# Pairing the state transposes and their additions in a software-pipelined Mamba and mixture-of-experts kernel, with the silu and softplus groups moved by a slot

## The chip, the cores and the metric

The kernel runs on one core of a Trainium2 chip. The metric is the device time of one execution in microseconds. All data are f32. The engines are named as in the profile: PE (TensorE, matrix products and transposes), PEld (its weight loads), DVE (VectorE), ACT (ScalarE), POOL (GpSimd) and SP (SyncE, which issues the transfers). Each runs its own list of instructions in order, and they wait for each other through semaphores.

## The reference

The input has 2 sequences of 4096 tokens of 256 values. One Mamba layer is followed by one mixture-of-experts layer, each with a layer norm before it, a layer norm behind it and a residual:

```
xz = einsum('bld,de->ble', layernorm(x), W_in); x_in, z = split(xz, 2)   # 512 channels each
u = silu(causal_conv4(x_in) + conv_b)
dt, B, C = split(u @ W_xproj, [16, 16, 16]);  delta = softplus(dt @ W_dt + b_dt)
h_t = exp(delta_t * A) * h_(t-1) + (delta_t * u_t) * B_t      # 512 channels x 16 states
y_t = sum over states of h_t * C_t
out = ((y + D_skip * u) * silu(z)) @ W_out;   x = x + layernorm(out)
...
x = x + layernorm(shared(x') + sum over the top 2 of 8 experts of coef * down(silu(gate) * up))
```

with x' the layer norm of x, 8 routed experts of width 128 and one shared expert of width 256 (two more blocks of 128, so 10 blocks f = 0 to 9).

## The kernel before

The tokens are cut into 16 chunks of T = 512, and a chunk into four quarters of 128 tokens. One pass of the loop over chunks has 64 slots (16 states times 4 blocks of 128 channels), and three chunks are in work in it: the scan of chunk s, the output projection and experts of chunk s - 1 (`ffn_part`), and the input projection, convolution, softplus and so on of chunk s + 1 (`prep_part`, `conv_part`). Every engine has its own loop over the slots t = 0 to 63. A table of slot numbers, written by hand, says in which slot an engine issues which piece, and so alone sets the order on each engine. Slots are places in these lists and no times: an engine may be a slot or more ahead of another, as far as the semaphores let it.

In each slot ACT makes one exponential d_a = exp(delta * A) (line 599), for the scan two slots later, since there are two PSUM banks for d_a. DVE runs one scan (line 757) for one state and 128 channels, and frees the bank. POOL makes d_bu for two slots at a time (line 1002).

The state h lies with channels on the partitions, and y is wanted with tokens there. So for each state n and quarter a (together q = 4n + a, 0 to 63 in a chunk) PE transposes four blocks of 128x128 into a PSUM bank `ht` (`transpose_state`, line 447), and DVE multiplies them by C and adds them to y_t (`add_state`, line 767). For q = 0 to 3 ACT does this instead (`first_state`, line 607, in its slots 5 to 8). There are two `ht` banks: the transposes of q wait for the addition of q - 2. Before the change PE transposes q in its slot q + 4, and DVE adds mostly one q in a slot. `LATER` names six slots with no addition and six, three slots on, with two.

Around this lie, in the order of a pass (the names are those of the table):
- y_t is transposed back (YD_PE, line 460), D_skip * u is added by DVE (YD_DVE), POOL multiplies by silu(z) (Y_GATE, line 1058) and PE projects (OUT_PE, line 471). DVE takes moments (O_STATS), adds the residual and takes moments again (X1_STATS). POOL makes the reciprocal deviation, ACT normalizes (line 616), PE transposes (X1T_PE, line 490) and ACT copies (line 656).
- PE projects the four blocks of x_in (XIN_PE, line 435). ACT takes the halo and the first tap (TAP0_ACT, lines 688, 692) and scales the taps of block 3 (line 700), DVE does the other taps of blocks 0 to 2 (CONV, line 924), POOL those of block 3 (line 1045), ACT the silu of u (SILU).
- The experts come in five pairs of blocks that start at PAIR_AT: two gates (line 509), then silu on ACT two slots later, the up products (line 516) three slots after the gates, the `hidden` products on POOL five slots after, the down products (line 536) later. An up product goes to the bank `ring` of its gate, which the silu frees. The last down product is in PE's slot 59, and DVE's moments of the expert layer's result (Y_STATS, slot 60) wait for it.
- DL_PE and DL_ACT are the product for delta and its softplus, Z_PE the product for z, CF_PE, CT_PE and XD_PE small ones. The next gate's bank is the one that a softplus frees.

Silu and softplus need another table on ACT than exp, so a group of them has an ACT_TABLE_LOAD ahead of it and one behind it.

Of the kernel before, what the change touches and what calls it, by code (L numbers as in the profile page):

```python
# [33 lines left out]
def mamba_moe_kernel(nc, x, w_in, conv_w, conv_b, w_xproj, w_dt, b_dt, a_log, d_skip, w_out,  # L34
# [10 lines left out]
    NT = T // P  # L45
    KM = DM // P
    J = DI // P
# [11 lines left out]
    with ExitStack() as ctx:  # L59
# [128 lines left out]


        SLOTS = NS * NT  # L190
        XIN_PE, TAP0_ACT, CONV = (5, 5, 8, 9), (5, 6, 9, 9), (7, 8, 11, 11)
        POOL_J, POOL_CONV = J - 1, 11
        YD_PE, YD_DVE, Y_GATE, OUT_PE = 3, 4, 5, (6, 6, 7, 7)
        O_STATS, X1_STATS, X1T_PE = 9, 10, 11
        PAIR_AT = (12, 21, 31, 41, 50)
        ROUTER_PE, ROUTE_DVE, ROUTE_EXP = 14, (15, 17, 18), 15
        XD_PE, CF_PE, CT_PE = 18, 20, 47
        DL_PE, DL_ACT = (27, 28, 37, 38), (29, 29, 39, 39)
        XA_STATS, XA_RSTD, XA_NORM = (31, 31, 41, 41), 43, 49
        DU_POOL = (58, 58, 60, 60)  # L200
        Z_PE, Y_STATS = (56, 57, 60, 61), 60
        SILU = {8: [("u", 0), ("u", 1)], 12: [("u", 2), ("u", 3)], 58: [("z", 0), ("z", 1)], 62: [("z", 2), ("z", 3)]}

        LATER = {13: 16, 22: 25, 28: 31, 32: 35, 42: 45, 51: 54}
        ADDS, todo = {}, iter(range(NT, SLOTS))
        for t in range(2 * NT + 1, SLOTS):
            count = 0 if t in LATER else 2 if t in LATER.values() else 1
            ADDS[t] = [next(todo) for _ in range(count)]

        def yd_bank(j):  # L210
            return RING[j] if j < 2 else DN[j - 2]
# [1 line left out]
        def added(c, q):  # L213

            if q < NT:
                return y_first.sem, y_first.at(c, q + 1)
            return add_c.sem, add_c.at(c, q - NT + 1)

        def gate_slot(f):
            return PAIR_AT[f // 2] + f % 2  # L220

        def silu_slot(f):
            return PAIR_AT[f // 2] + 2

# [6 lines left out]
        def down_slot(f):  # L231

            if f // 2 + 1 < len(PAIR_AT):
                return PAIR_AT[f // 2 + 1] + (2, 5)[f % 2]
            return gate_slot(f) + 8
# [41 lines left out]
        def parts(lo):  # L277

            return exists(lo), exists(lo - 1), exists(lo + 1)

        def exists(chunk):
            return 0 <= chunk < CHUNKS
# [116 lines left out]
        def _(pe):  # L399
# [4 lines left out]
            def body(s, lo, r):  # L404
                with_scan, ffn, prep = parts(lo)
                if lo == 1:
                    pe.wait_ge(ffn_ld.sem, FFN_LOADS)
                for t in range(SLOTS):
                    if with_scan and t >= NT:
                        transpose_state(s, t - NT)  # L410
                    if ffn and t < NT // 2:
                        transpose_state(s - 1, SLOTS - NT + 2 * t)
                        transpose_state(s - 1, SLOTS - NT + 2 * t + 1)
                    if ffn:
                        ffn_part(s, lo, t)
                    if prep:
                        prep_part(s, lo, 1 - r, t)
# [21 lines left out]
            def transpose_state(c, q):  # L439

                n, a = q // NT, q % NT
                if a == 0:
                    pe.wait_ge(scan.sem, scan.at(c, (n + 1) * J))
                before, p = (c, q - HTS) if q >= HTS else (c - 1, q - HTS + SLOTS)
                pe.wait_ge(*added(before, p))
                for j in range(J):
                    last = nc.tensor.transpose(HT[q % HTS][:, j * P:(j + 1) * P],  # L447
                                               H[:, (NS * c + n) % HS, j, a * P:(a + 1) * P], IDN[:, :])
                last.then_inc(ht_full.sem, 1)
# [92 lines left out]
            def prep_part(s, lo, o, t):  # L542
# [29 lines left out]
                if t == CT_PE:  # L572
# [7 lines left out]
                    last.then_inc(full["ct"].sem, 1)  # L580

            run(body)

        @block.scalar
        def _(act):
# [91 lines left out]
            def prep_part(s, lo, o, t):  # L677
# [6 lines left out]
                for j in range(J):  # L684
                    if t == TAP0_ACT[j]:
# [9 lines left out]
                        if j == POOL_J:  # L695
                            act.wait_ge(o_full.sem, o_full.at(c - 2))
                            act.wait_ge(conv_last.sem, conv_last.at(c - 1))
                            for k in range(TAPS - 1):
                                back = TAPS - 1 - k
                                nc.scalar.activation(YD[:, k, back:], ring_bank("xin", j)[:, 0:T - back], ACT.Copy,  # L700
                                                     scale=CW[:, j, k:k + 1]).then_inc(scaled.sem, 1)
                for what, k in SILU.get(t, ()):
                    if what == "u":
# [29 lines left out]
        def _(dve):  # L733
# [15 lines left out]
            def scan_step(s, r, n, j):  # L749
                dve.wait_ge(ex.sem, ex.at(s, n * J + j + 1))  # L750
                if j % 2 == 0:
                    dve.wait_ge(bu.sem, bu.at(s, 2 * n + j // 2 + 1))
                if j == 0:

                    dve.wait_ge(ht_full.sem, ht_full.at(s, NT * (n - HS + 1)))
                    dve.wait_ge(carry.sem, carry.at(s, n - HS + 1))
                nc.vector.tensor_tensor_scan(H[:, (NS * s + n) % HS, j, :], DA[(n * J + j) % DAS][:, :],  # L757
                                             BU[:, (2 * n + j // 2) % 4, j % 2, :],
                                             CARRY[:, r, n, j:j + 1], ALU.mult, ALU.add)\
                  .then_inc(scan.sem, 1)  # L760

            def add_state(c, r, q):

                n, a = q // NT, q % NT
                dve.wait_ge(ht_full.sem, ht_full.at(c, q + 1))
                dve.wait_ge(*added(c, q - NT))
                nc.vector.scalar_tensor_tensor(YT[:, a, :], HT[q % HTS][:, :], CT[:, r, a, n:n + 1],  # L767
                                               YT[:, a, :], ALU.mult, ALU.add).then_inc(add_c.sem, 1)
# [9 lines left out]
            def moments(w, c, a, tile):  # L778
                nc.vector.bn_stats(ST[w][:, a, :], tile).then_inc(stats[w].sem, 1)  # L779
# [14 lines left out]
            def add_stream_y(c, a):  # L794

                dve.wait_ge(rstd["y"].sem, rstd["y"].at(c))
                nc.vector.scalar_tensor_tensor(XR[:, a, :], dn(a), RS["y"][:, a:a + 1], XR[:, a, :],  # L797
                                               ALU.mult, ALU.add).then_inc(resid["y"].sem, 1)

            def dn(a):  # L800
                return DN[a // 2][:, (a % 2) * DM:(a % 2 + 1) * DM]

            def body(s, lo, r):
                with_scan, ffn, prep = parts(lo)
                o = 1 - r
                for t in range(SLOTS):
                    if with_scan:
                        scan_step(s, r, t // J, t % J)
                    if ffn:
                        ffn_part(s - 1, o, t, s if with_scan else s - 1)  # L810
                    if prep:
                        conv_part(s + 1, o, t)
                    if with_scan and t in ADDS:
                        for q in ADDS[t]:
                            add_state(s, r, q)
                    for a in range(NT):
                        if exists(lo + 2) and t == XA_STATS[a]:
                            dve.wait_ge(xa_ld.sem, xa_ld.at(s + 2))
                            moments("xa", s + 2, a, XA[:, a, :])
                            if a == NT - 1:  # L820
                                moments_end("xa", s + 2)
                    if ffn and t == 0:
                        add_state(s - 1, o, SLOTS - NT - 1)
                    if exists(lo - 2) and t == 0:
                        for a in range(NT):
                            add_stream_y(s - 2, a)
                    if ffn and t in (1, 2):
                        for a in (2 * t - 2, 2 * t - 1):
                            add_state(s - 1, o, SLOTS - NT + a)

            def over(t):
                return t.unsqueeze(2).to_broadcast([P, NT, E])
# [80 lines left out]
            def conv_part(c, o, t):  # L913
                if t == CONV[POOL_J]:
                    dve.wait_ge(scaled.sem, scaled.at(c))
                    conv_head(c, o, POOL_J, conv_last)
                for j in range(POOL_J):
                    if t == CONV[j]:
                        conv_head(c, o, j, conv)
                        for i in range(TAPS - 1):  # L920
                            k = TAPS - 2 - i
                            back = TAPS - 1 - k
                            dve.wait_ge(conv.sem, conv.at(c, TAPS * j + i + 1))
                            nc.vector.scalar_tensor_tensor(U[:, o, j, back:], ring_bank("xin", j)[:, 0:T - back],  # L924
                                                           CW[:, j, k:k + 1], U[:, o, j, back:],
                                                           ALU.mult, ALU.add).then_inc(conv.sem, 1)

            run(body)

        @block.gpsimd  # L930
# [181 lines left out]
```

## Time and profile before

| | |
|---|---|
| median of 3 runs | 2518.28 us (2516.38 to 2519.62) |
| the profiled execution | 2519.9 us, its span 2518.1 us |
| PE busy | 2151.6 us, 85% |
| DVE busy | 2231.6 us, 89% |
| ACT busy | 1677.0 us, 67% |
| POOL busy | 1934.7 us, 77% |
| mean granted TensorE clock | 0.887 |

The span runs from the first to the last instruction, and the execution's own time is 1.8 us more. A matmul's end is modelled, so PE's busy time is not PE at its peak. Each number of idle time comes with the instruction that ended it.

### The profile page before, as it was taken

How to read it: one execution, taken by the hardware profiler on the slowest of the kernel's cores; microseconds unless marked ns; L12 is line 12 of the kernel's file. 1: busy time of each engine (PE TensorE's matmuls, PEld its weight loads, DVE VectorE, ACT ScalarE, POOL GpSimd, SP SyncE). 2: the span in 40 equal slices, each digit the busy share in tenths (PEclk: the TensorE clock that was granted, in tenths of full speed). 3: DMA queues.
4: the chain of work that ended last, by engine and by line, in shares of the span. 5: the costliest groups of instructions: out<-in, count | busy, mean ns of one | idle time of the engine just before them, and what ended most of it. 6: DMA issues, size and time to landing. Idle time of an engine off the chain costs nothing. (4 is left out here: it accounts for less than half of the span.)

```text
span 2518.1 us, 29889 instructions
## 1 busy us (share of the span) xinstructions
PE 2151.6 (85%) x8960; PEld 1374.5 (55%) x8960; DVE 2231.6 (89%) x3192; ACT 1677.0 (67%) x2437; POOL 1934.7 (77%) x1598
## 2 busy tenths in 40 slices
PE   5578989889898988989889898988989898896878
PEld 2345565556555555555645555565555556564554
DVE  2899998999999999999999999999999999988961
ACT  4556776677667767777676777667767676764532
POOL 3577887978778797878879788797878879686843
PEclk8758989999899899989889898998989898997979
DMA  4111211111112111111211221121112111111201
GB/s 120 38 34 43 63 55 48 56 56 52 49 59 61 47 54 52 59 51 56 63 47 45 61 60 51 55 64 43 47 51 68 51 56 55 43 51 42 63 22 42
DMA packets 92945, 134.25 MB, mean 53 GB/s; under 512 B 12000, under 2 KB 42976, under 8 KB 92784
## 3 DMA queue, kind: packets, MB, share of 16 engines
q1 hardware_dynamic: 92784, 132.34, 17.4%
q8 instruction: 72, 1.18, 0.2%
q14 instruction: 89, 0.73, 0.1%
HBM read 123.13 MB, written 9.18 MB: 53 GB/s over the span
## 5 line engine op out<-in xcount | busy, mean ns | idle before, releaser
L757 DVE TENSOR_TENSOR_SCAN h<-d_a,carry,d_bu 128x512 f32<-128x512 f32 x1024 | 1290.9, 1273 | 60.7 <-ACT d_a L599 60.7
L1002 POOL TENSOR_TENSOR d_bu<-delta_u,b_rows 128x1024 f32<-128x1024 f32 x512 | 1201.4, 2360 | 5.0 <-DMA b_rows<-b_rows_hbm 0.5
L599 ACT ACTIVATE d_a<-delta,a_neg 128x512 f32<-128x512 f32 x1024 | 696.4, 689 | 573.3 <-DVE h L757 571.1
L447 PE MATMUL ht<-ident,h 128*128 128x128 f32 x4096 | 700.6, 303 | 275.5 <-DVE y_t L767 263.2
L447 PEld LDWEIGHTS ht<-ident,h 128*128 128x128 f32 x4096 | 533.3, 154 | 668.8 <-DVE y_t L767 351.8
L767 DVE SCALAR_TENSOR_TENSOR y_t<-ht,c_t,y_t 128x512 f32<-128x512 f32 x960 | 694.0, 733 | 47.6 <-PE ht L447 46.5
L1065 POOL TENSOR_TENSOR hidden<-silu_gate,up 128x512 f32<-128x512 f32 x160 | 203.8, 1274 | 211.5 <-ACT up L669 115.4
L509 PE MATMUL ring<-x_t,w_gate_sb 128*128 128x512 f32 x640 | 354.5, 684 | 1.1 <-ACT x_t L656 1.0
L516 PE MATMUL ring<-x_t,w_up_sb 128*128 128x512 f32 x640 | 312.3, 613 | 0.0
L536 PE MATMUL dn<-w_down_sb,hidden 128*128 128x256 f32 x1280 | 303.0, 380 | 1.3 <-POOL hidden L1070 1.3
L536 PEld LDWEIGHTS dn<-w_down_sb,hidden 128*128 128x128 f32 x1280 | 231.3, 190 | 30.9 <-issue 3.1
L599 ACT ACT_TABLE_LOAD x167 | 214.3, 1283 | 2.9
L509 PEld LDWEIGHTS ring<-x_t,w_gate_sb 128*128 128x128 f32 x640 | 130.5, 226 | 102.6 <-issue 100.6
L1051 POOL TENSOR_TENSOR carry<-h,one 128x4 f32<-128x4 f32 x256 | 51.7, 202 | 164.2 <-DVE h L757 164.2
L1070 POOL TENSOR_TENSOR hidden<-hidden,coef_rows 128x512 f32<-128x512 f32 x128 | 162.9, 1273 | 10.0
L516 PEld LDWEIGHTS ring<-x_t,w_up_sb 128*128 128x128 f32 x640 | 113.9, 197 | 83.5 <-issue 83.3
L669 ACT ACTIVATE up<-ring 128x512 f32<-128x512 f32 x160 | 94.6, 591 | 87.4 <-PE ring L516 87.4
L779 DVE BATCH_NORM_STATS2 stats_o<-dn 128x6 f32<-128x256 f32 x128 | 46.4, 419 | 93.9 <-PE dn L536 75.2
L435 PE MATMUL ring<-z_buf,w_in_sb 128*128 128x512 f32 x256 | 126.0, 627 | 2.8 <-DVE u L924 1.8
L553 PE MATMUL ring<-z_buf,w_in_sb 128*128 128x512 f32 x256 | 122.9, 605 | 0.3 <-ACT c_t L727 0.3
L471 PE MATMUL dn<-w_out_sb,y_d 128*128 128x256 f32 x512 | 120.5, 390 | 0.9 <-POOL y_d L1058 0.9
L924 DVE SCALAR_TENSOR_TENSOR u<-ring,conv_w_sb,u 128x511 f32<-128x511 f32 x144 | 107.8, 749 | 5.1
(110 smaller groups left out, 2003.1 us busy)
## 6 DMA issues: line engine op xcount, KB each, us to landing
b_rows<-b_rows_hbm SPq DMA_DIRECT2D x256, 256.0 KB, 3.5
coef_rows<-coef_rows_hbm SPq DMA_DIRECT2D x128, 256.0 KB, 3.5
xa<-L_attn_x_in SPq DMA_DIRECT2D x16, 512.0 KB, 3.9
xr<-L_attn_x_in SPq DMA_DIRECT2D x16, 512.0 KB, 3.9
out<-xr SPq DMA_DIRECT2D x16, 512.0 KB, 3.1
w_in_sb<-L_attn_W_in_in SPq DMA_DIRECT2D x1, 1024.0 KB, 6.4
w_gate_sb<-L_ffn_experts_gate_in SPq DMA_DIRECT2D x2, 512.0 KB, 4.7
w_up_sb<-L_ffn_experts_up_in SPq DMA_DIRECT2D x2, 512.0 KB, 5.5
```

The costliest lines, as they stand in the source:

```text
L435: last = nc.tensor.matmul(ring_bank("xin", j)[:, :], WIN[:, k, j * P:(j + 1) * P], XT[:, k, :], start=(k == 0), stop=(k == KM - 1))
L447: last = nc.tensor.transpose(HT[q % HTS][:, j * P:(j + 1) * P], H[:, (NS * c + n) % HS, j, a * P:(a + 1) * P], IDN[:, :])
L509: last = nc.tensor.matmul(bank[:, :], WG[:, k, f, :], X1T[:, k, :], start=(k == 0), stop=(k == KM - 1))
L516: last = nc.tensor.matmul(bank[:, :], WU[:, k, f, :], X1T[:, k, :], start=(k == 0), stop=(k == KM - 1))
L536: last = nc.tensor.matmul(DN[a // 2][:, (a % 2) * DM:(a % 2 + 1) * DM], HF[:, f % 2, a * P:(a + 1) * P], WD[:, f, :], start=(f == 0 and a ...
L553: last = nc.tensor.matmul(ring_bank("z", j)[:, :], WIN[:, k, DI + j * P:DI + (j + 1) * P], XT[:, k, :], start=(k == 0), stop=(k == KM - 1))
L599: nc.scalar.activation(DA[i % DAS][:, :], DL[:, r, j, :], ACT.Exp, scale=ANEG[:, j, n:n + 1]).then_inc(ex.sem, 1)
L757: nc.vector.tensor_tensor_scan(H[:, (NS * s + n) % HS, j, :], DA[(n * J + j) % DAS][:, :], BU[:, (2 * n + j // 2) % 4, j % 2, :], CARRY[:, ...
L767: nc.vector.scalar_tensor_tensor(YT[:, a, :], HT[q % HTS][:, :], CT[:, r, a, n:n + 1], YT[:, a, :], ALU.mult, ALU.add).then_inc(add_c.sem, 1)
L1002: nc.gpsimd.tensor_tensor(BU[:, (2 * n + h) % 4, :, :], DU[:, 2 * h:2 * h + 2, :], BB[:, n % 2, :].unsqueeze(1).to_broadcast([P, 2, T]), A ...
L1065: nc.gpsimd.tensor_tensor(HF[:, f % 2, :], TG[:, f % 2, :], UP[:, f % 2, :], ALU.mult).then_inc(hf.sem, 1)
L1070: nc.gpsimd.tensor_tensor(HF[:, f % 2, :], HF[:, f % 2, :], CB[:, e % 2, :], ALU.mult)\
```

## The change

Transposes and additions are now done for two q at a time. DVE adds q = t - 6 and t - 5 in each even slot t from 10 on, and q = 58 and 59 at the end of slot 63. PE transposes the two in the odd slot before. The last four of a chunk (q = 60 to 63) are added in slots 0 and 1 of the next pass instead of 1 and 2. The steps from the transposes of y_t up to X1T_PE, and the convolution's, move one slot up. The silu of u2, u3 moves from slot 12 to 11. The middle pairs of experts, and the softplus groups, move one slot down, so that their silus and softplus fall in even slots. The same instructions are issued as before, none is added or removed.

```
-        XIN_PE, TAP0_ACT, CONV = (5, 5, 8, 9), (5, 6, 9, 9), (7, 8, 11, 11)
+        XIN_PE, TAP0_ACT, CONV = (4, 4, 7, 8), (4, 5, 8, 8), (6, 7, 10, 10)
...
-        PAIR_AT = (12, 21, 31, 41, 50)
+        PAIR_AT = (12, 22, 32, 42, 50)
...
-        LATER = {13: 16, 22: 25, 28: 31, 32: 35, 42: 45, 51: 54}
-        ADDS, todo = {}, iter(range(NT, SLOTS))
-        for t in range(2 * NT + 1, SLOTS):
-            count = 0 if t in LATER else 2 if t in LATER.values() else 1
-            ADDS[t] = [next(todo) for _ in range(count)]
+        ADDS = {t: (t - NT - 2, t - NT - 1) for t in range(NT + 2, SLOTS, 2)}
+        ADDS[SLOTS] = (SLOTS - NT - 2, SLOTS - NT - 1)
+        ADDS_LATE = {0: (SLOTS - NT, SLOTS - NT + 1), 1: (SLOTS - NT + 2, SLOTS - NT + 3)}
...
-                    if with_scan and t >= NT:
-                        transpose_state(s, t - NT)
-                    if ffn and t < NT // 2:
-                        transpose_state(s - 1, SLOTS - NT + 2 * t)
-                        transpose_state(s - 1, SLOTS - NT + 2 * t + 1)
+                    for q in ADDS.get(t + 1, ()):
+                        if with_scan:
+                            transpose_state(s, q)
+                    for q in ADDS_LATE.get(t, ()):
+                        if ffn:
+                            transpose_state(s - 1, q)
```

On PE, around the third pair of experts, before. `ht<-ident,h` x4 is one transpose of a q, `x_dbl` the product for delta, and 128x512 x2 one gate or one up product:

```order
L568 MATMUL ring<-x_dbl,w_dt_sb 128x512
L447 MATMUL ht<-ident,h 128x128 x12
L509 MATMUL ring<-x_t,w_gate_sb 128x512 x2
L447 MATMUL ht<-ident,h 128x128 x4
L509 MATMUL ring<-x_t,w_gate_sb 128x512 x2
L447 MATMUL ht<-ident,h 128x128 x4
L536 MATMUL dn<-w_down_sb,hidden 128x256 x4
L447 MATMUL ht<-ident,h 128x128 x4
L516 MATMUL ring<-x_t,w_up_sb 128x512 x2
L447 MATMUL ht<-ident,h 128x128 x4
L516 MATMUL ring<-x_t,w_up_sb 128x512 x2
```

The same place after (lines are one less there):

```order
L567 MATMUL ring<-x_dbl,w_dt_sb 128x512
L446 MATMUL ht<-ident,h 128x128 x8
L508 MATMUL ring<-x_t,w_gate_sb 128x512 x2
L446 MATMUL ht<-ident,h 128x128 x8
L508 MATMUL ring<-x_t,w_gate_sb 128x512 x2
L535 MATMUL dn<-w_down_sb,hidden 128x256 x4
L446 MATMUL ht<-ident,h 128x128 x8
L515 MATMUL ring<-x_t,w_up_sb 128x512 x4
L446 MATMUL ht<-ident,h 128x128 x8
```

Two transposes now stand together ahead of two products, where one stood ahead of each, and the second gate has two more transposes ahead of it instead of one.

On PE, around the output projection (`w_out_sb`) and the x_in products (`w_in_sb`), before:

```order
L460 MATMUL dn<-ident,y_t 128x128 x8
L447 MATMUL ht<-ident,h 128x128 x8
L435 MATMUL ring<-z_buf,w_in_sb 128x512 x4
L447 MATMUL ht<-ident,h 128x128 x4
L471 MATMUL dn<-w_out_sb,y_d 128x256 x8
L447 MATMUL ht<-ident,h 128x128 x4
L471 MATMUL dn<-w_out_sb,y_d 128x256 x8
L447 MATMUL ht<-ident,h 128x128 x4
L435 MATMUL ring<-z_buf,w_in_sb 128x512 x2
```

After:

```order
L459 MATMUL dn<-ident,y_t 128x128 x8
L434 MATMUL ring<-z_buf,w_in_sb 128x512 x4
L446 MATMUL ht<-ident,h 128x128 x8
L470 MATMUL dn<-w_out_sb,y_d 128x256 x16
L446 MATMUL ht<-ident,h 128x128 x8
L434 MATMUL ring<-z_buf,w_in_sb 128x512 x4
```

The transposes of q = 2 and 3, which stood ahead of and between the two halves of the output projection, now stand behind all of it.

On ACT at the same place, before. `y_t<-ht,c_t` is `first_state`, here of q = 2 and 3, `u<-u` the silu of u0 and u1:

```order
L607 ACTIVATE y_t<-ht,c_t 128x512
L599 ACTIVATE d_a<-delta,a_neg 128x512
L607 ACTIVATE y_t<-ht,c_t 128x512
L708 ACT_TABLE_LOAD
L708 ACTIVATE u<-u 128x512 x2
L599 ACT_TABLE_LOAD
L599 ACTIVATE d_a<-delta,a_neg 128x512
L688 ACTIVATE halo<-ring 128x3
L692 ACTIVATE u<-ring,conv_b_sb,conv_w_sb 128x509
```

After:

```order
L606 ACTIVATE y_t<-ht,c_t 128x512
L598 ACTIVATE d_a<-delta,a_neg 128x512
L606 ACTIVATE y_t<-ht,c_t 128x512
L687 ACTIVATE halo<-ring 128x3
L691 ACTIVATE u<-ring,conv_b_sb,conv_w_sb 128x509
...
L699 ACTIVATE y_d<-ring,conv_w_sb 128x511
L707 ACT_TABLE_LOAD
L707 ACTIVATE u<-u 128x512 x2
L598 ACT_TABLE_LOAD
L598 ACTIVATE d_a<-delta,a_neg 128x512
```

The taps of x_in's blocks 2 and 3, which stood behind the silu group, now stand ahead of it.

## Rows read from the trace of the kernel before

**Rows 1.** Waits of DVE, 786.5 to 1083.5 us: total us, times, longest.

```profile
DVE y_t L767 <- PE ht L447: 5.6, 13, 1.4
DVE h L757 <- ACT d_a L599: 4.3, 8, 1.6
DVE stats_o L779 <- PE dn L536: 3.9, 2, 2.0
DVE r_small L843 <- PE dn L498: 1.9, 2, 1.5
```

**Rows 2.** Timeline of DVE, 1011 to 1014 us: start, us.

```profile
1011.48 0.72 DVE L767 SCALAR_TENSOR_TENSOR y_t<-ht,c_t,y_t 128x512 f32<-128x512 f32 x1
1012.12 1.27 DVE L757 TENSOR_TENSOR_SCAN h<-d_a,carry,d_bu 128x512 f32<-128x512 f32 x1
1013.31 1.38 DVE L767 SCALAR_TENSOR_TENSOR y_t<-ht,c_t,y_t 128x512 f32<-128x512 f32 x2
```

**Rows 3.** Waits of DVE, 1010 to 1033 us.

```profile
DVE y_t L767 <- PE ht L447: 2.7, 5, 1.4
```

**Rows 4.** Timeline of PE, 1015 to 1026 us: start, us; idle before and what ended it.

```profile
1015.00 3.62 PE L509 MATMUL ring<-x_t,w_gate_sb 128*128 128x512 f32 x4
...
1023.58 0.60 PE L447 MATMUL ht<-ident,h 128*128 128x128 f32 x4
1024.02 1.88 PE L516 MATMUL ring<-x_t,w_up_sb 128*128 128x512 f32 x4
1025.73 0.60 PE L447 MATMUL ht<-ident,h 128*128 128x128 f32 x4
```

**Rows 5.** Stretches: from:to, length, busy by engine, granted clock, DMA.

```profile
1013.30:1020.10 6.80, 6.01 (x13) 3.34 (x14) 6.80 (x10) 5.35 (x7) 6.80 (x4) 0.50 0.13 45
...
1085.00:1088.40 3.40, 2.82 (x12) 2.42 (x12) 3.40 (x7) 2.02 (x4) 3.40 (x4) 0.50 0.22 62
1088.40:1091.80 3.40, 1.31 (x8) 0.84 (x8) 3.40 (x5) 2.15 (x4) 3.16 (x7) 1.00 0.50 169
```

**Rows 6.** Timeline of PE, 1085 to 1104 us.

```profile
1085.43 1.11 PE L447 MATMUL ht<-ident,h 128*128 128x128 f32 x4 [1.11 <-DVE y_t L767]
1086.34 1.92 PE L425 MATMUL ring<-ident,xa 128*128 128x128 f32 x8
...
1100.08 3.62 PE L471 MATMUL dn<-w_out_sb,y_d 128*128 128x256 f32 x16
```

**Rows 7.** Timeline of ACT, 1104 to 1119 us.

```profile
1104.77 0.67 ACT L607 ACTIVATE y_t<-ht,c_t 128x512 f32<-128x512 f32 x1
1105.45 1.28 ACT L708 ACT_TABLE_LOAD   x1
1106.75 1.15 ACT L708 ACTIVATE u<-u 128x512 f32<-128x512 f32 x2
...
1116.56 2.08 ACT L616 ACTIVATE z_buf<-xr,mean_rstd_x,rstd_x 128x256 f32<-128x256 f32 x4 [1.46 <-POOL mean_rstd_x L990]
```

**Rows 8.** Timeline of DVE: scans of slots 3 and 17 in two passes.

```profile
942.20 2.45 DVE L757 TENSOR_TENSOR_SCAN h<-d_a,carry,d_bu 128x512 f32<-128x512 f32 x2
...
983.43 1.28 DVE L757 TENSOR_TENSOR_SCAN h<-d_a,carry,d_bu 128x512 f32<-128x512 f32 x1
...
1091.84 2.45 DVE L757 TENSOR_TENSOR_SCAN h<-d_a,carry,d_bu 128x512 f32<-128x512 f32 x2
...
1126.09 1.28 DVE L757 TENSOR_TENSOR_SCAN h<-d_a,carry,d_bu 128x512 f32<-128x512 f32 x1 [1.58 <-ACT d_a L599]
...
1131.29 1.27 DVE L757 TENSOR_TENSOR_SCAN h<-d_a,carry,d_bu 128x512 f32<-128x512 f32 x1
```

**Rows 9.** Timelines of DVE and PE, from slot 50's scan to the moments.

```profile
1052.98 1.27 DVE L757 TENSOR_TENSOR_SCAN h<-d_a,carry,d_bu 128x512 f32<-128x512 f32 x1
...
1060.68 1.88 PE L516 MATMUL ring<-x_t,w_up_sb 128*128 128x512 f32 x4
...
1075.57 1.43 DVE L779 BATCH_NORM_STATS2 stats_o<-dn 128x6 f32<-128x256 f32 x4 [1.95 <-PE dn L536]
```

More of the change, by code:

```diff
@@ L190, in mamba_moe_kernel @@
         SLOTS = NS * NT
-        XIN_PE, TAP0_ACT, CONV = (5, 5, 8, 9), (5, 6, 9, 9), (7, 8, 11, 11)
-        POOL_J, POOL_CONV = J - 1, 11
-        YD_PE, YD_DVE, Y_GATE, OUT_PE = 3, 4, 5, (6, 6, 7, 7)
-        O_STATS, X1_STATS, X1T_PE = 9, 10, 11
-        PAIR_AT = (12, 21, 31, 41, 50)
[L196 to L199, printed above, removed]
+        XIN_PE, TAP0_ACT, CONV = (4, 4, 7, 8), (4, 5, 8, 8), (6, 7, 10, 10)
+        POOL_J, POOL_CONV = J - 1, 10
+        YD_PE, YD_DVE, Y_GATE, OUT_PE = 2, 3, 4, (5, 5, 6, 6)
+        O_STATS, X1_STATS, X1T_PE = 8, 9, 10
+        PAIR_AT = (12, 22, 32, 42, 50)
+        ROUTER_PE, ROUTE_DVE, ROUTE_EXP = 14, (16, 18, 19), 16
+        XD_PE, CF_PE, CT_PE = 18, 20, 48
+        DL_PE, DL_ACT = (28, 29, 38, 39), (30, 30, 40, 40)
+        XA_STATS, XA_RSTD, XA_NORM = (32, 32, 42, 42), 44, 49
         DU_POOL = (58, 58, 60, 60)
         Z_PE, Y_STATS = (56, 57, 60, 61), 60
-        SILU = {8: [("u", 0), ("u", 1)], 12: [("u", 2), ("u", 3)], 58: [("z", 0), ("z", 1)], 62: [("z", 2), ("z", 3)]}
-        LATER = {13: 16, 22: 25, 28: 31, 32: 35, 42: 45, 51: 54}
-        ADDS, todo = {}, iter(range(NT, SLOTS))
-        for t in range(2 * NT + 1, SLOTS):
-            count = 0 if t in LATER else 2 if t in LATER.values() else 1
-            ADDS[t] = [next(todo) for _ in range(count)]
+        SILU = {8: [("u", 0), ("u", 1)], 11: [("u", 2), ("u", 3)], 58: [("z", 0), ("z", 1)], 62: [("z", 2), ("z", 3)]}
+        ADDS = {t: (t - NT - 2, t - NT - 1) for t in range(NT + 2, SLOTS, 2)}
+        ADDS[SLOTS] = (SLOTS - NT - 2, SLOTS - NT - 1)
+        ADDS_LATE = {0: (SLOTS - NT, SLOTS - NT + 1), 1: (SLOTS - NT + 2, SLOTS - NT + 3)}
         def yd_bank(j):
@@ L812, in body @@
                         conv_part(s + 1, o, t)
-                    if with_scan and t in ADDS:
-                        for q in ADDS[t]:
-                            add_state(s, r, q)
+                    if exists(lo - 2) and t == 0:
+                        for a in range(NT):
+                            add_stream_y(s - 2, a)
+                    for q in ADDS.get(t, ()):
+                        if with_scan and q >= NT:
+                            add_state(s, r, q)
+                    if with_scan and t == SLOTS - 1:
+                        for q in ADDS[SLOTS]:
+                            add_state(s, r, q)
+                    for q in ADDS_LATE.get(t, ()):
+                        if ffn:
+                            add_state(s - 1, o, q)
                     for a in range(NT):
@@ L821, in body @@
                                 moments_end("xa", s + 2)
[L822 to L829, printed above, removed]
             def over(t):
```

## The prediction

> **What bounds the kernel.** I read the waits of DVE first, over two passes of the loop in the steady part, 297 us long. DVE has the largest busy share in the table, and whoever keeps it waiting sets the time. It waits 15.7 us in two passes in four ways: for transposes (5.6), for exponentials (4.3), for the last down product (3.9), for the router (1.9), 25 times in all [rows 1]. Busy neighbours on DVE overlap by 0.08 us (a scan of 1.27 us is followed 1.19 us after its start, an addition of 0.72 us after 0.64 [rows 2]), so a wait costs 0.08 us more than its row says: (15.7 + 25 x 0.08) / 2 = about 8.9 us a pass. The other 139.6 us of a pass are DVE's own work. The change touches none of it, and pairing saves nothing of it: the two additions of slot 31 take 1.38 us together, 0.64 and a last one of 0.74 [rows 2]. All that can be won is part of 8.9 us, in some 15 passes that have both experts and scans, 134 us in all.
>
> The waits are local. I then read the timelines around each, to find on whom DVE waits there and what is late on that engine.
>
> **Third pair of experts (slots 31 to 38): gain 2.6 us a pass.** Here DVE waits 2.7 us in five places for transposes [rows 3], 3.1 us with the lost overlap. The reason stands in PE's rows: the pair's first gate runs at the granted clock 0.50 (1.2 GHz) and takes 3.62 us, where an up product of the same shape takes 1.88 us at 1.00 [rows 4, 5]. At full clock PE repeats a transpose (0.44 us to the next start) and a product (1.71) in 2.15 us [rows 4], and DVE a scan and an addition in 1.83 [rows 2]: each slot with a product costs PE 0.32 us of its lead. That lead is the time from the addition that frees the bank to the addition that needs it, 2 scans and 1 addition (3.0 us) less 0.2 of latency and 0.6 of transposing, 2.2 us. Six slots in a row with products use 1.9 of it. The low clock adds up to 3.4 us, and the sum goes over the lead by 3.1.
>
> After the change the lead of a pair is the same 2.2 us. But a pair is transposed ahead of the second gate, where one was, and the pair ahead of the up products belongs to additions that come after them. I follow it in us from the end of slot 24's scan, DVE unhindered but for 0.3 us that slot 24's silu group costs (below): the additions of slots 28, 30, 34, 36 and 38 start at 7.6, 11.3, 19.2, 22.9 and 26.9. PE: down product till 8.9, delta product, pair, delta product till 11.7, pair at 12.1 to 13.0. The gate's bank is freed by the softplus of slot 30: 11.3 + exponential 0.8 + table 1.3 + softplus 0.7 = 14.1. So the gate runs from 14.2. If the clock is low for 3.4 us around it, it ends at about 17.1; pair and second gate till 19.9, down product 21.6, pair 22.5 (wanted at 22.9), up products till 26.0, pair, whose first is there at 26.6 (wanted at 26.9). No transpose is late. What stays is 0.3 us behind slot 34's silu group. Gain: 3.1 less 0.3, rounded down to 2.6 for what I may have missed. If the low stretch lasts 6.8 us, as now [rows 5], DVE waits some 1.6 and the gain is 1.5. The ends are 1.1 and 2.8.
>
> **Silu groups in even slots: no change.** A group holds ACT for two table loads of 1.28 us and two silus (1.15) [rows 7], with an exponential before and behind it 5.2 us from a scan's end to the exponential for the third scan on. DVE has two scans and four additions in that time, 2.4 + 2.6 = 5.0. That holds in an even slot now, and held before by `LATER`; 0.3 us each. The sum so takes 1.28 us for a table. By the Trainium skill, "ScalarE: Activation LUTs", section on what ACT_TABLE_LOAD costs, a switch takes a load of about 1283 ns and a drain of about 1380 ns; by that a group would hold ACT 2.8 us longer, and DVE would wait some 3 us at each. The trace disagrees: the silu starts 0.02 us behind the 1.28 us of the load [rows 7].
>
> **Start of a pass (slots 0 to 17): loss 1.0 us.** The steps up to X1T_PE move one slot up, and so do the last additions, so against each other they stay. I count from X, the end of the addition of q = 63, which is the scan of slot 3 before and of slot 2 after. Before, slot 17's scan starts at X + 41.2 in one pass and 39.5 in the next [rows 8]; with the one scan more that now lies between (1.2) that is 42.4 and 40.7, mean 41.5.
> After: y_t is transposed till X + 3.7, the x_in products till 7.2, pair till 8.1, the 16 matmuls of the output projection twice (3.6 each) [rows 6] till 15.3. Only then come the transposes of q = 2 and 3. ACT, which now is done with `first_state` of q = 3 at 1105.44 or X + 13.6 [rows 7, 8], waits for q = 2 till 15.8 and is done with both at 17.8. Then, now ahead of the silus, the taps: block 2 at 18.8, block 3, whose product ends at 19.5, at 20.5, three scalings till 22.2, two tables and two silus till 26.0, the exponential for slot 11 at 26.7 (wanted at 27.3). The four normalizing instructions (2.08 us), for which ACT waited 1.46 us on POOL before [rows 7], could start at 24.2 and start at 26.7. So the exponential for slot 12 is 0.8 us late, and the one for slot 14, behind the copies of x1 and the silu group of slot 11, 2.6 us late, where now the one for slot 15 is 1.6 late [rows 8]. POOL's reciprocal deviation is no longer hidden by an addition, 0.3. The wait for the router (0.9 a pass) goes, since PE is through at 39.3 and DVE asks at 40.5. Slot 17's scan starts at X + 42.5: 1.0 us more than 41.5. If PE runs the x_in products and the projection at the low clock, ACT is as much later: up to 1.7 us more. If ACT catches up, the loss is 0. So 0 to 2.7.
>
> **Second pair of experts: loss 0.3 us.** The routing on DVE now lies a slot later, and between the end of the x_dbl product and the third gate PE has 5.5 us with little but transposes, 3.6 before. A low clock is likelier there; with 6.8 us of it DVE waits 0.8 us in place of 0.3. Half of that. Bounds 0 and 0.6.
>
> **Slots 50 to 60: loss 0.35 us.** PE is behind from the gates on, and DVE waits 1.95 us for the last down product [rows 9]. From the start of the first up product to the moments are 14.9 us, PE without a break. After, the same products with the same six transposes follow. The up product starts 7.7 us behind slot 50's scan now [rows 9]; after, the first gate waits for the bank of c_t, copied on ACT a slot later, till 1.1 and ends at 2.85; pair 3.7, gate 5.45, down product 7.2, pair 8.05. So the wait grows by 0.35.
>
> **Sum.** - 2.6 + 1.0 + 0.3 + 0.35 = - 0.95 us a pass, 15 passes: - 14. The passes without experts or without scans (the first, and the tail) stay, since nothing waits differently there. Against the profiled execution's own 2519.9 us, 1.6 above the median of 2518.3, that is 2506, and for the median 2504.
>
> **Rivals.** Differences below 0.2%, 5 us, can't be told from no change in this kernel.
> 1. ACT decides (slower). The mechanism is that of the start of a pass: `first_state` behind the whole output projection. ACT has 0.6 us to spare at slot 11's exponential. If ACT is 0.95 us later than I have it, all of the gain is gone; at the upper bound of 2.7 us the sum is + 0.75 us, + 11, 2530. For it: ACT's row of waits there is already short, 1.46 us. Against: the projection ran at full clock in the rows [rows 6]. Chance 0.2.
> 2. The clock. Pairs leave PE idle for 2.6 us at a time in slots without products, where one transpose in each slot left 1.2. If the low stretches last 6.8 us at the second, third and fourth pair (the fourth costs nothing now), the sum is - 1.5 + 1.1 + 0.6 + 1.0 + 0.35 = + 1.55, + 23, 2541. For it: the low stretch of 6.8 us at the third pair [rows 5]. Against: after the change the pair of transposes runs up to the gate, so the pause is shorter. Chance 0.15. [...]
> 3. ACT isn't late: the taps and the silus fit, and the start costs nothing. Sum - 1.95, - 29, 2489. Chance 0.2.
> 4. The waits only move: the third pair gives 1.6 and the rest takes it. 2514 to 2523. Chance 0.17.
> My forecast, 2494 to 2513: chance 0.28.
>
> **How the numbers follow.** Faster: 0.28 + 0.2 and a little of the others, 0.48. Same 0.17. Slower 0.35. The range leaves out half of rival 3 below and half of rival 2 above: 2486 to 2536. Within the forecast itself: 2494 to 2513.
>
> **What would show it.** In the profile of the changed kernel: DVE's waits for transposes in two passes fall from 5.6 to under 1; those for exponentials rise from 4.3 to about 8; those for the router go to near 0; the ones for the last down product rise to 4.5. ACT's idle time before the normalizing (POOL's mean_rstd_x) goes to 0, and ACT waits for `ht` some 2.8 us a pass instead of under 1. The prediction is wrong if slot 17's scan comes more than 43.5 us behind X, if the clock is low for 6.8 us at the third and fourth pair, or if transposes stay late there at full clock.

## The result and the profile after

| | before | after |
|---|---|---|
| median | 2517.98 us (2516.38 to 2519.62, 4 runs) | 2477.78 us (2475.04 to 2478.14, 4 runs) |
| span of the profiled execution | 2518.1 us | 2475.9 us |
| mean granted TensorE clock | 0.887 | 0.918 |
| DVE busy | 2231.6 us | 2221.5 us |

The ratio is 0.9838, with a 95% interval of 0.9821 to 0.9855. The change made the kernel 40 us faster, and the two spans differ by 42.2 us. I had forecast 14 us, and the time lies below my range.

DVE's waits after the change come first, over two passes, 293.5 us long; columns as in [rows 1], its counterpart.

```profile
DVE h L756 <- ACT d_a L598: 7.7, 12, 2.3
DVE stats_o L778 <- PE dn L535: 5.4, 2, 2.7
DVE xr L790 <- POOL rstd_o L974: 0.6, 2, 0.3
DVE y_t L766 <- PE ht L446: 0.4, 2, 0.2
```

Transposes went from 5.6 to 0.4, the router from 1.9 to nothing. The exponentials went from 4.3 to 7.7, the last down product from 3.9 to 5.4 (4.5 expected), POOL's 0.6 is new. That was the expected pattern. The twelve steady passes give half of the 42.2 us of the two spans; I took the length of each pass from the start of its first scan to that of the next pass, and that of the last one up to the start of its own last scan:

| stretch | before | after | difference |
|---|---|---|---|
| up to the first scan | 61.4 | 60.6 | -0.8 |
| first pass with scans (no experts) | 132.7 | 130.2 | -2.5 |
| second | 146.2 | 144.5 | -1.7 |
| twelve passes, mean of one | 148.45 | 146.79 | -1.66, -19.9 in all |
| the one behind them | 149.6 | 146.0 | -3.6 |
| last pass with scans | 145.1 | 133.5 | **-11.6** |
| tail (experts alone) | 101.8 | 99.8 | -2.0 |

**The start of a pass.** The timeline of ACT in a steady pass after the change, where X is 928.99 (compare [rows 7]):

```profile
945.09 0.69 ACT L606 ACTIVATE y_t<-ht,c_t 128x512 f32<-128x512 f32 x1 [3.12 <-PE ht L446]
...
948.97 0.17 ACT L687 ACTIVATE halo<-ring 128x3 f32<-128x3 f32 x1 [0.87 <-PE ring L434]
949.03 0.78 ACT L691 ACTIVATE u<-ring,conv_b_sb,conv_w_sb 128x509 f32<-128x509 f32 x1
949.71 1.83 ACT L699 ACTIVATE y_d<-ring,conv_w_sb 128x509 f32<-128x509 f32 x3
951.55 1.28 ACT L707 ACT_TABLE_LOAD   x1
952.85 1.15 ACT L707 ACTIVATE u<-u 128x512 f32<-128x512 f32 x2
954.02 1.28 ACT L598 ACT_TABLE_LOAD   x1
955.31 0.69 ACT L598 ACTIVATE d_a<-delta,a_neg 128x512 f32<-128x512 f32 x1
```

And DVE's scans behind it:

```profile
958.61 1.28 DVE L756 TENSOR_TENSOR_SCAN h<-d_a,carry,d_bu 128x512 f32<-128x512 f32 x1 [0.69 <-ACT d_a L598]
...
964.74 1.28 DVE L756 TENSOR_TENSOR_SCAN h<-d_a,carry,d_bu 128x512 f32<-128x512 f32 x1 [2.30 <-ACT d_a L598]
```

Each step is within 0.5 us of the walk in the prediction: copies of the first state from X + 16.1 (15.8 there), the silus and both table loads through at X + 26.3 (26.0), waits of 0.69 and 2.30 us (0.8 and 2.6). Slot 17's scan starts at 971.23, X + 42.2.

**The third pair.** The timeline of PE has the pair's two gates, and below it stand the stretches around them (from:to, length, busy, granted clock, DMA). In the kernel before the first gate took 3.62 us [rows 4] and the second 2.31.

```profile
1002.21 1.98 PE L508 MATMUL ring<-x_t,w_gate_sb 128*128 128x512 f32 x4 [0.76 <-ACT delta L721]
1004.03 1.08 PE L446 MATMUL ht<-ident,h 128*128 128x128 f32 x8
1004.95 1.88 PE L508 MATMUL ring<-x_t,w_gate_sb 128*128 128x512 f32 x4
```

```profile
997.80:1001.20 3.40, 3.40 (x20) 1.00 0.23 82
1001.20:1004.60 3.40, 2.64 (x12) 1.00 0.17 58
```

The granted clock is 1.00 (2.4 GHz) in these stretches, and the gates take 1.98 and 1.88 us. PE pauses 0.76 us ahead of the gate; before, the low level of 0.50 covered 6.8 us there [rows 5].

**The last pass with scans.** DVE's waits in it, before the change and after it:

```profile
DVE stats_o L779 <- PE dn L471: 6.8, 1, 6.8
DVE y_t L767 <- PE ht L447: 4.6, 9, 1.4
DVE r_small L843 <- PE dn L498: 2.6, 1, 2.6
DVE h L757 <- ACT d_a L599: 1.1, 4, 0.4
DVE stats_o L779 <- PE dn L536: 0.5, 1, 0.5
```

```profile
DVE h L756 <- ACT d_a L598: 1.8, 5, 1.0
DVE stats_o L778 <- PE dn L470: 1.7, 1, 1.7
DVE stats_o L778 <- PE dn L535: 1.2, 1, 1.2
DVE h L756 <- issue: 0.3, 1, 0.3
DVE xr L790 <- POOL rstd_o L974: 0.3, 1, 0.3
```

They sum to 15.6 and 5.3 us. The largest is the wait for the output projection, 6.8 us against 1.7. PE's timeline before, with the stretches around the projection:

```profile
2287.32 1.11 PE L447 MATMUL ht<-ident,h 128*128 128x128 f32 x4 [3.11 <-ACT y_t L607]
2288.22 6.13 PE L471 MATMUL dn<-w_out_sb,y_d 128*128 128x256 f32 x16
2294.19 0.60 PE L447 MATMUL ht<-ident,h 128*128 128x128 f32 x4
2294.62 3.62 PE L471 MATMUL dn<-w_out_sb,y_d 128*128 128x256 f32 x16
```

```profile
2284.90:2288.30 3.40, 0.98 (x5) 0.73 0.80 189
2288.30:2291.70 3.40, 3.40 (x10) 0.50 0.42 135
```

And after:

```profile
2255.56 7.17 PE L470 MATMUL dn<-w_out_sb,y_d 128*128 128x256 f32 x32 [0.81 <-POOL y_d L1058]
```

```profile
2256.30:2259.70 3.40, 3.40 (x17) 1.00 0.72 150
```

Before, the transposes of quarter 2 stood ahead of the projection and waited 3.11 us for ACT's copy of the first state. The clock fell to 0.50, and the first half took 6.13 us. After, the projection comes first, starts on POOL's gating and runs at 1.00. A steady pass has the x_in products there, and no such stop.

### The profile page after: what moved, and what is told of

Same layout as the page of the kernel before. It is cut to its first block and busy times, and to the rows that moved or that the text cites. A ratio compares the mean times of both kernels' runs of the same rounds, so it can differ in the third digit from the quotient of the medians.

```text
span 2475.9 us, 29889 instructions
## 1 busy us (share of the span) xinstructions
PE 2078.7 (84%) x8960; PEld 1345.9 (54%) x8960; DVE 2221.5 (90%) x3192; ACT 1665.0 (67%) x2437; POOL 1931.3 (78%) x1598
## 5 line engine op out<-in xcount | busy, mean ns | idle before, releaser
L756 DVE TENSOR_TENSOR_SCAN h<-d_a,carry,d_bu 128x512 f32<-128x512 f32 x1024 | 1262.3, 1267 | 83.4 <-ACT d_a L598 83.0
L446 PE MATMUL ht<-ident,h 128*128 128x128 f32 x4096 | 612.9, 293 | 136.2 <-DVE y_t L766 132.9
L446 PEld LDWEIGHTS ht<-ident,h 128*128 128x128 f32 x4096 | 501.9, 150 | 381.6 <-issue 144.4
L766 DVE SCALAR_TENSOR_TENSOR y_t<-ht,c_t,y_t 128x512 f32<-128x512 f32 x960 | 666.6, 735 | 3.8 <-PE ht L446 3.3
L508 PE MATMUL ring<-x_t,w_gate_sb 128*128 128x512 f32 x640 | 329.5, 642 | 22.3 <-ACT delta L721 21.0
L515 PE MATMUL ring<-x_t,w_up_sb 128*128 128x512 f32 x640 | 294.0, 602 | 27.4 <-ACT silu_gate L664 27.3
L535 PEld LDWEIGHTS dn<-w_down_sb,hidden 128*128 128x128 f32 x1280 | 237.1, 190 | 66.7 <-issue 35.2
L508 PEld LDWEIGHTS ring<-x_t,w_gate_sb 128*128 128x128 f32 x640 | 121.5, 211 | 125.6 <-issue 92.8
L489 PE MATMUL dn<-ident,z_buf 128*128 128x128 f32 x128 | 34.6, 448 | 109.2 <-ACT z_buf L615 109.2
L470 PE MATMUL dn<-w_out_sb,y_d 128*128 128x256 f32 x512 | 113.3, 379 | 1.8 <-POOL y_d L1058 1.8
```

Source lines behind the costliest of these rows:

```text
L508: last = nc.tensor.matmul(bank[:, :], WG[:, k, f, :], X1T[:, k, :], start=(k == 0), stop=(k == KM - 1))
L515: last = nc.tensor.matmul(bank[:, :], WU[:, k, f, :], X1T[:, k, :], start=(k == 0), stop=(k == KM - 1))
L535: last = nc.tensor.matmul(DN[a // 2][:, (a % 2) * DM:(a % 2 + 1) * DM], HF[:, f % 2, a * P:(a + 1) * P], WD[:, f, :], start=(f == 0 and a ...
```

## The experiments

All were timed beside the kernel before. Its median was 2516.75 us beside the first four runs, 2514.11 beside those of the router, the first state, the last pass and slot 60, and 2517.94 beside those of the taps and the combinations. The first four take the change apart into three pieces: pairing (transposes and additions two at a time), the front (XIN_PE to X1T_PE, CONV, second silu group a slot sooner), and the middle (PAIR_AT, ROUTE, CT, DL and XA in even slots).

**Pairing alone.** The changed kernel with front and middle in their slots of before:

```diff
...
-        YD_PE, YD_DVE, Y_GATE, OUT_PE = 2, 3, 4, (5, 5, 6, 6)
+        YD_PE, YD_DVE, Y_GATE, OUT_PE = 3, 4, 5, (6, 6, 7, 7)
...
-        PAIR_AT = (12, 22, 32, 42, 50)
+        PAIR_AT = (12, 21, 31, 41, 50)
...
```

> Only the pairing of transposes and additions; all other steps in the slots of before. Theory L (each wait follows from its place): the groups of slots 23, 29, 33, 39 and 43 are in odd slots now, with two additions instead of four until the exponential is wanted, so each waits about 1.3 us longer (those with moments beside them less): 4 to 6 us a pass more than after, 2530 to 2580 us, slower than before. Rival F (the gain comes from the start of the pass being a slot sooner): about the time of before, 2510 to 2525. Rival C (pairing alone raises the clock and removes the wait at the third pair): 2480 to 2500.

Measured: 2536.41 us, ratio 1.0078 (1.0064 to 1.0093). DVE's waits in two passes:

```profile
DVE h L756 <- ACT d_a L598: 13.2, 14, 1.5
DVE stats_o L778 <- PE dn L535: 5.4, 2, 2.7
DVE r_small L843 <- PE dn L497: 1.8, 2, 0.9
DVE xr L790 <- POOL rstd_o L974: 0.6, 2, 0.3
```

Pairing alone removes every wait for transposes, but with silu groups in odd slots the exponentials cost more than that.

**Everything but the front.** The changed kernel with the front in its slots of before:

```diff
-        XIN_PE, TAP0_ACT, CONV = (4, 4, 7, 8), (4, 5, 8, 8), (6, 7, 10, 10)
+        XIN_PE, TAP0_ACT, CONV = (5, 5, 8, 9), (5, 6, 9, 9), (7, 8, 11, 11)
...
-        O_STATS, X1_STATS, X1T_PE = 8, 9, 10
+        O_STATS, X1_STATS, X1T_PE = 9, 10, 11
...
```

> The changed kernel with the start of the pass (transposes of y_t to x1, x_in products, convolution, silu of u2 and u3) back in its old slots. Theory L: the silu group of slot 12 is even again and costs 0.3 us instead of the 2.4 us that slot 11's does, and the 0.9 us before slot 12 shrinks, so a steady pass is 1 to 3 us shorter; the last pass with scans loses part of its 11 us: 2440 to 2475. Rival F: the start a slot sooner is what gave the gain, so it is lost: 2495 to 2520.

Measured: 2449.64 us, ratio 0.9735 (0.9721 to 0.9749), 28 us less than the changed kernel. A steady pass takes 144.8 us. The exponentials' wait is 3.2 us in two passes, where the changed kernel has 7.7:

```profile
DVE h L756 <- ACT d_a L598: 3.2, 11, 0.9
```

So, beside pairing and the even slots, the sooner front loses 28 us.

**Everything but the middle.** The changed kernel with PAIR_AT, ROUTE, CT, DL and XA as before.

> The changed kernel with the middle pairs of experts, routing, softplus and the input's moments back in their old slots, so their groups are in odd slots. Theory L: five groups wait about 1.3 us longer, 4 to 6 us a pass: 2530 to 2570. Rival C (the pairing itself is enough, the slots of the groups do not matter): 2475 to 2490.

Measured: 2555.57 us, ratio 1.0155 (1.014 to 1.0169), exponentials 18.3 us in two passes. With pairing in place, the even slots are worth 78 us here (sooner front), and 87 between the two runs above (front as before).

**The front alone,** in the kernel before.

> The kernel of before (one addition a slot, the middle as before) with only the start of the pass a slot sooner. Theory L: the wait at the third pair (2.9 us a pass) stays; the steady passes stay within 1 us; the last pass with scans loses part of its 7 us wait for the projection: 2500 to 2525. Rival F: most of the 40 us: 2475 to 2490.

Measured: 2571.89 us, ratio 1.0221 (1.0177 to 1.0264), outside every range given. The four executions fall into two near 2561 us (clock 0.878) and two near 2583 (0.874), and the profile is of one of the latter. Its waits in two passes (of 153.6 us each) include one that nobody expected, the router's:

```profile
DVE h L757 <- ACT d_a L599: 7.9, 10, 3.0
DVE r_small L843 <- PE dn L498: 6.4, 2, 3.2
```

PE's timeline in one of them shows the router's product behind a pause:

```profile
850.48 1.09 PE L447 MATMUL ht<-ident,h 128*128 128x128 f32 x4 [2.57 <-DVE y_t L767]
851.36 3.42 PE L498 MATMUL dn<-router_sb,x_t 128*128 128x8 f32 x16
```

The 16 matmuls take 3.42 us at a granted clock of 0.50, and 1.85 at 1.00 in the kernel before:

```profile
978.06 1.85 PE L498 MATMUL dn<-router_sb,x_t 128*128 128x8 f32 x16
```

**The last pass with scans in these four.** It took 145.1 us before the change and 133.5 after. It takes 139.3 with pairing alone, 134.9 with everything but the front, 137.4 with everything but the middle and 140.8 with the front alone, and DVE's wait for the projection, 6.8 us before, is 1.4, 3.1, 1.7 and 1.6 us in them. So pairing alone gives 5.8 of the 11.6 us and the even slots another 3.9 to 4.4. The front alone gives 4.3, but with the rest in place it adds only 1.4.

**The front, and the router a slot later,** in the kernel before:

```diff
...
-        ROUTER_PE, ROUTE_DVE, ROUTE_EXP = 14, (15, 17, 18), 15
+        ROUTER_PE, ROUTE_DVE, ROUTE_EXP = 14, (16, 18, 19), 16
...
```

> The kernel before with the front of a pass a slot sooner, as in the earlier run of the front alone, and with DVE's router steps and ACT's exponential for them a slot later too (16, 18, 19 and 16). The front alone took 2571.9 us and had a wait of 3.2 us a pass for the router's product. Theory A (the front sooner brings DVE to slot 15 sooner than PE can have the router's product, and that wait is what made it slower): the router wait falls below 0.3 us, a pass gets 2.5 to 3.2 us shorter, and the kernel takes 2523 to 2535 us, still 5 to 18 us slower than before, because the waits for the exponentials (4.0 us a pass against 2.15) stay. Theory B (something else in PE's order, its clock above all, made the passes longer): the router wait moves to the next product and the kernel stays above 2550 us.

Measured: four executions, one of 2534.45 us (clock 0.900) and three from 2579.82 to 2581.79 (clock 0.875). The profile is of the first, and in it the router's wait fell from 6.4 to 2.2 us in two passes. That is 1.1 us a pass, where theory A expected under 0.3, though a pass takes 150.2 us, 3.4 less than with the front alone, and the time of this one execution lies in the range of theory A. The other three are no faster than the front alone, and no profile shows where their time went. Inconclusive: the code alone doesn't fix the clock in this order of work.

**First state between the halves of the projection.** In the changed kernel PE transposes quarters 2 and 3 a slot sooner:

```diff
-                    for q in ADDS.get(t + 1, ()):
+                    for q in {6: ADDS[NT + 4], 7: ()}.get(t, ADDS.get(t + 1, ())):
```

> The changed kernel, but the transposes of quarters 2 and 3 of the state stand between the two halves of the output projection instead of behind it. Theory A (the front of a pass became costly because ACT's copies of the first state, `y_t<-ht`, now wait 3.1 us behind the whole projection, and ACT then reaches the exponentials for slots 12 and 14 late): the copies start some 3 us sooner, DVE's waits for d_a at slots 11 and 13 (0.93 and 2.39 us a pass) fall to about 0 and 1.6, a pass gets 1.7 us shorter, and the kernel takes 2445 to 2460 us. Theory B (ACT is late because of the convolution's first taps and the silu group standing a slot sooner, whatever the projection does): the waits stay within 0.5 us and the kernel takes 2470 to 2485 us. If a wait for the projection takes the place of the exponentials' (the second half comes later by the transposes, 1.1 us), stats_o waits by L470 appear and the time is 2460 to 2475 us.

Measured: 2478.38 us, ratio 0.9859 (0.9839 to 0.9878): no gain on the changed kernel. ACT's timeline shows why:

```profile
942.57 0.67 ACT L606 ACTIVATE y_t<-ht,c_t 128x512 f32<-128x512 f32 x1
945.60 0.69 ACT L598 ACTIVATE d_a<-delta,a_neg 128x512 f32<-128x512 f32 x1 [2.35 <-DVE h L756]
...
947.90 0.18 ACT L687 ACTIVATE halo<-ring 128x3 f32<-128x3 f32 x1 [1.00 <-PE ring L434]
...
949.61 0.17 ACT L687 ACTIVATE halo<-ring 128x3 f32<-128x3 f32 x1 [0.87 <-PE ring L434]
```

The copy no longer waits (its pass starts 0.65 us later, so 942.57 is 3.2 us sooner). But the taps still wait for x_in's last product, which PE can only have done behind the projection, and everything from there on is where it was. Theory A falls.

**Taps a slot later.** The changed kernel, where x_in and the projection keep their sooner slots:

```diff
-        XIN_PE, TAP0_ACT, CONV = (4, 4, 7, 8), (4, 5, 8, 8), (6, 7, 10, 10)
+        XIN_PE, TAP0_ACT, CONV = (4, 4, 7, 8), (4, 5, 9, 9), (6, 7, 11, 11)
...
```

> The changed kernel, but ACT's first taps of pieces 2 and 3, the additions of the other taps on DVE and POOL, and the second silu group stand where the kernel before has them, a slot later (9 and 9, 11 and 11, 11, 12); the output projection and x_in's products keep their sooner slots. Theory A (ACT is late for slots 12 and 14 because those taps stand ahead of the first silu group and of the exponential, and wait for x_in's last product, at 948.97 in pass 6): the exponential of slot 12 starts some 4 us sooner, DVE's waits for d_a at slots 11 and 13 fall from 3.3 to under 1.2 us a pass, a pass gets 1.7 to 2.4 us shorter, and the kernel takes 2440 to 2453 us. Theory B (the output projection's sooner slot is what costs, the pass with front and second half back having 144.8 us because of it): the waits stay above 2.5 us a pass and the kernel takes 2465 to 2480 us.

Measured: 2501.21 us, ratio 0.9939 (0.9922 to 0.9955), 23 us more than the changed kernel, outside both ranges. The waits for exponentials did go at slots 11 and 13, to come back by 1.3 us at 14 and 16, but a new one stands at the convolution's additions, on DVE and, behind it, ACT:

```profile
965.43 0.35 DVE L909 SCALAR_TENSOR_TENSOR u<-ring,conv_w_sb,head 128x3 f32<-128x3 f32 x2 [3.41 <-ACT y_d L699]
```

```profile
960.15 2.08 ACT L615 ACTIVATE z_buf<-xr,mean_rstd_x,rstd_x 128x256 f32<-128x256 f32 x4 [1.34 <-POOL mean_rstd_x L990]
962.14 0.15 ACT L687 ACTIVATE halo<-ring 128x3 f32<-128x3 f32 x1
```

In slot 9 the normalizing (X1_STATS = 9) comes ahead of the taps, and it waits for POOL's shift. In the changed kernel the taps stand ahead of it, in the one with the whole front back too (taps 9, normalizing 10). So the taps are squeezed between x_in's product and the normalizing. With pairing and even slots in place, the two orders that keep the front in one piece (2449.64 and 2477.78 us) are the faster ones.

**The last pass alone.** The kernel before, with the transposes of quarters 2 and 3 behind the projection in the last pass with scans and nowhere else:

```diff
-                    if with_scan and t >= NT:
+                    behind = ffn and not prep
+                    if with_scan and t >= NT and not (behind and t in (6, 7)):
+                        if behind and t == 8:
+                            transpose_state(s, 2)
+                            transpose_state(s, 3)
                         transpose_state(s, t - NT)
```

> The kernel before, changed in one pass alone, the last one with scans: the state's transposes of quarters 2 and 3 stand behind the whole output projection on PE instead of ahead of each half. Theory A (in that pass PE stops 3.11 us for ACT ahead of the projection, which then runs at a granted clock of 0.5, and DVE waits 6.8 us for it): PE doesn't stop there, the projection's first half takes less than 5 us, DVE's wait for it falls from 6.8 to between 1.5 and 3.5 us, and the kernel takes 2510 to 2515 us, 3 to 6 us less than the kernel before. Theory B (the clock is low there whatever stands ahead, or the router's wait takes up what the projection gives back): the pass keeps its 145.1 us within 1 us and the kernel takes 2516 to 2519 us.

Measured: 2510.91 us (10 runs), ratio 0.9981 (0.9963 to 0.9999). That pass takes 140.9 us in place of 145.1, and all but three of the others are as they were within 0.1 us (those three, near the sixth, are 3.3 us shorter together without a change in their code, one of them by 2.3). PE's timeline, and DVE's waits in the pass:

```profile
2279.33 7.17 PE L475 MATMUL dn<-w_out_sb,y_d 128*128 128x256 f32 x32 [0.64 <-POOL y_d L1062]
```

```profile
DVE y_t L771 <- PE ht L451: 5.7, 12, 1.4
DVE r_small L847 <- PE dn L502: 3.6, 1, 3.6
DVE h L761 <- ACT d_a L603: 0.9, 3, 0.4
DVE stats_o L783 <- PE dn L475: 0.6, 1, 0.6
```

The projection runs at 1.00, its wait falls from 6.8 to 0.6, and the router (2.6 to 3.6) and the transposes (4.6 to 5.7) take 2.1 of it back. The wait fell further than theory A expected (1.5 to 3.5 us). The rest came out as it says: PE no longer stops for ACT, and the time is in its range. So the stop ahead of the projection, and the clock behind it, cost this pass 4.2 us. That is one execution's figure. The medians of the two kernels differ by 3.2 us, with an interval from 0.3 to 9.

**The wait at slot 60.** The changed kernel with the moments of the experts' residual, and POOL's step behind them, two slots later:

```diff
-        Z_PE, Y_STATS = (56, 57, 60, 61), 60
+        Z_PE, Y_STATS = (56, 57, 60, 61), 62
...
-                    if ffn and t == 60:
+                    if ffn and t == Y_STATS:
```

> The changed kernel, but the moments of the experts' residual stand in slot 62 instead of 60 on DVE, and POOL's step behind them too. Theory A (the 2.7 us that DVE waits at slot 60 for the last down product are paid on the path): the wait goes, a pass gets 2.3 to 2.8 us shorter, and the kernel takes 2435 to 2445 us. Theory B (the shift that POOL works out and ACT's last exponentials come later in their turn, so the wait only moves to the first slots of the next pass): 2465 to 2480 us, with a new wait of over 2 us a pass at slots 62 to 3.

Measured: 2442.93 us, ratio 0.9718 (0.9701 to 0.9734), 35 us less than the changed kernel. The wait for the last down product is gone, 0.6 us a pass for a transpose stands in its place, and a steady pass takes 144.5 us, 2.3 less. Theory A holds.

**Combinations.** The kernel with the whole front back and slot 62:

> The kernel with the whole front of a pass back in its slots of before (2449.6 us) and the moments of the experts' residual in slot 62. If the two gains add up (the changed kernel gained 34.9 us by slot 62): 2412 to 2420 us. If the slot-60 wait covered the first exponentials of the next pass, or these take it over: 2425 to 2440 us.

Measured: **2417.83 us**, ratio 0.9606 (0.9591 to 0.962), a steady pass of 142.7 us. The gains add up within 3 us (31.8 us by slot 62 here, 35 in the changed kernel), and this beats both kernels.

The changed kernel with the taps a slot later and slot 62:

> The changed kernel with its taps a slot later, as in the run of these alone, and the moments of the experts' residual in slot 62. If both gains add: 2405 to 2420 us. If the sooner output projection costs something of its own, it is slower than the kernel with the whole front back and slot 62 by 5 us or more.

Measured: 2477.37 us, ratio 0.9842 (0.9828 to 0.9857), far above the range for both gains, as the run of the taps alone had already lost time. It is 60 us slower than with the whole front back. DVE waits 3.4 us a pass ahead of the additions, as without slot 62, and slot 62 gives 24 us.

The same, with the first state between the halves of the projection:

> As the one with taps a slot later and slot 62, but with the transposes of quarters 2 and 3 between the halves of the output projection, so that ACT's copies of the first state come 3 us sooner. With the taps out of the way the copies are the last thing ahead of the silu group: if they still make an exponential late, this gives 0.3 to 1 us a pass, 5 to 15 us less than without it. If no exponential waits there any more, the two are within 3 us.

Measured: 2477.64 us, ratio 0.9844 (0.9829 to 0.9859). The same time: with the additions' wait in place, sooner copies of the first state give nothing.

## Why the prediction was wrong, step by step

**The step that failed** is the sentence "The passes without experts or without scans (the first, and the tail) stay, since nothing waits differently there", together with "15 passes" of one price. I counted the last pass with scans as a steady one. It isn't: it has no x_in products, DVE waited 15.6 us in it, and the change gave 11.6 us there in place of 0.95. The run of that pass alone shows 4.2 us of it to be the projection's stop and low clock. The causes of the other 7.4 no run separates. The rows of waits have 5.8 of them: transposes 4.6 to 0, router 2.6 to 0, less 0.7 for each of exponentials and last down product. The first pass with scans, which I had at nothing, gave 2.5 (its rows have 2.4 us of waits for transposes before and none after), and the pass ahead of the last, in which no new input is prepared for the next but one, gave 3.6. The start and the tail gave 2.8 together, but the run of the last pass alone has 59.2 and 99.2 us for code that took 61.4 and 101.8 in the kernel before, so that can be scatter.

**Third pair: right.** Predicted 2.6 us a pass, measured 2.65. In the timelines, each start of a DVE instruction compared with the usual spacing of such a pair, slots 35 to 38 lost 2.93 us before and lose 0.28 after. I had kept 3.4 us of low clock in it, with no transpose late; in the stretches after the clock isn't low at all.

**Silu groups in even slots: right.** Still 0.28 us at each of slots 26, 36, 46 and 54. "No change" held only against a table with its `LATER`: with pairing, odd groups cost 78 to 87 us more than even ones.

**Start of a pass: 1.0 predicted, 0.7 measured,** with slot 17's scan at X + 42.2 (42.5 predicted) against 41.5. The walk was right in its times and wrong in one reason, that of rival 1: not the copies of the first state but x_in's last product, behind the projection on PE, holds ACT. Moving the copies changed nothing.

**Second pair: 0.3 predicted, nothing measured.** The silu group waits 0.28 there as before, and no transpose is late. **Slots 50 to 60: 0.35 predicted, 0.3 measured** (the last product +0.7, transposes of slots 57 to 59 -0.4).

The terms measured sum to -2.65 + 0.7 + 0.3 = -1.65, and the steady pass gave 1.66 in place of 0.95: two losses, at the start and at the second pair, that I had each 0.3 too large. Over the second pass and the twelve behind it that is 9.3 us more than forecast, the pass ahead of the last gives 2.7, the last 10.6, the first with scans 2.5, and start and tail 2.8: the 28 us between the 14 forecast and the 42.2 of the spans. None of my three signs of being wrong appeared: the scan of slot 17 came ahead of X + 43.5, and at the third and fourth pair the clock was at 1.00 and no transpose late. All three look at steady passes alone, and so could not show the error.

Rival 2 (more low clock) went the wrong way: the mean granted clock rose from 0.887 to 0.918, and passes that had taken 149.6 and 147.3 us by turns now take 146.8 each.

## What to carry to other kernels

Read every kind of pass of a loop by itself, the last one above all: one list of waits over each would have shown 15.6 us where a steady pass has 7.9. When work is regrouped, follow what PE does in the pause ahead of each product; in the last pass a stop of 3.1 us cost 4.2 by itself and by the clock behind it. Most of a wait of a late instruction was had here by moving the instruction (2.3 of 2.7 us at slot 60), while moving a step that stands between two producers (the taps) by itself lost 23 us. And take a change apart: without its front this one would have been 28 us faster.

## What the runs showed of the hardware

In the same program the clock isn't always the same: with the front and the router moved, three executions ran at a mean granted clock near 0.875 and one at 0.900, 45 us apart. Small products pay for the clock almost as much as large ones: the router's 16 matmuls with 8 columns take 3.42 us at 0.50 and 1.85 at 1.00, a gate 3.62 and 1.88. And the level rose behind transposes alone: from 1085.0 to 1088.4 us in the kernel before PE had twelve of them and no other matmul, at 0.50, and the next stretch has 1.00 [rows 5, 6].
